# Staging of the weights before the first tile: double-buffered operand loads, two queues for the diagonal blocks, two weight matrices loaded later

## What is computed

```python
# layer 1: x = x + attn(layernorm(x))
mixed = silu(causal_depthwise_conv(x @ W_qkv.T, conv_w))      # K = 4 taps, 3072 channels
q, k, v = split(mixed);  z = x @ W_z.T
beta = sigmoid(x @ W_b.T);  g = -exp(A_log) * softplus(x @ W_a.T + dt_bias)
q = l2norm(q) / 8;  k = l2norm(k)
S = S * exp(g_t) + outer(k_t, v_t * beta_t);  o_t = q_t @ S    # per head, over time
out = (o * rsqrt(mean(o*o) + 1e-6) * silu(z)) @ W_out.T
# layer 2: x = x + ffn(layernorm(x))
def _unfold_tt(G1, G2):                                        # 512 x 512
    W = jnp.einsum('abcd,cefg->abefdg', G1, G2)
    return W.reshape(OUT_FEATURES, IN_FEATURES)
out_real = x_real @ W_real.T - x_imag @ W_imag.T + bias_real
out_imag = x_real @ W_imag.T + x_imag @ W_real.T + bias_imag
```

## Time and profile before

| what | us |
|---|---|
| runs (2): median, lowest, highest | 2968.16, 2960.76, 2975.57 |
| profiled execution: its own time | 2974.58 |
| its span on the slowest core (core 3) | 2973.0 |
| spans of the other cores | 2932.4 to 2961.1 |
| TensorE, matmuls busy | 1213.4 (41%) |
| VectorE (DVE) busy | 707.4 (24%) |
| ScalarE (ACT) busy | 342.2 (12%) |

### The profile page before, as it was taken

The page is one execution under the profiler, slowest core; times in us unless marked ns, Lnnn a source line. Parts: engine busy times, 40 slices in busy tenths (PEclk is TensorE's granted clock), DMA queues, the critical chain, the costliest instruction groups (busy, mean ns, idle before and its releaser), DMA issues.

```text
span 2973.0 us, 17447 instructions; the slowest of 8 cores (2932.4 to 2973.0 us)
## 1 busy us (share of the span) xinstructions
PE 1213.4 (41%) x5440; PEld 478.3 (16%) x5440; DVE 707.4 (24%) x1023; ACT 342.2 (12%) x570; POOL 131.1 (4%) x223
## 2 busy tenths in 40 slices
PE   0000072451634616614444733443852443762444
PEld 0000021211202213101122201111311111311111
DVE  0112312413214033022223022223112323202322
ACT  0000020020110201201110211111211111111111
POOL 1111100000000000000000000000000000000000
PEclk9999985655755657556566755665755666855656
DMA  9432202012030120121111101101011011012001
GB/s 162 64 85 92 88 18 22 18 39 8 22 29 18 39 1 18 47 5 18 18 18 39 23 25 4 35 19 39 11 36 6 18 34 34 13 41 5 18 18 25
DMA packets 138104, 94.79 MB, mean 32 GB/s; under 512 B 121003, under 2 KB 121776, under 8 KB 138016
## 3 DMA queue, kind: packets, MB, share of 16 engines
q0 software_dynamic: 44224, 39.15, 11.4%
q1 hardware_dynamic: 93792, 54.54, 6.7%
HBM read 99.76 MB, written 11.67 MB: 37 GB/s over the span
## 4 chain that ended last, share of the span: by engine, by line
PE 40%; DVE 19%; DMA 15%; ACT 10%; issue 8%; DVEq 3%; another core or an unknown queue 2%; POOL 2%; ACTq 0%; POOLq 0%; SPq 0%
PE ps L276 33%; DMA s_gamb<-scr 5%; PE psS L276 3%; DMA s_eaq<-scr 3%; ACT s_mixed L276 3%; PE psT L276 3%; DVE s_dsb L276 3%; DVE s_bn L276 3%; DVEq L275 2%; DVE s_Sall L276 2%; ACT L276 2%; DVE s_x2a L276 2%; ACT s_dsb L276 2%; DMA s_z<-p2i 2%
## 5 line engine op out<-in xcount | busy, mean ns | idle before, releaser
L276 PE MATMUL ps<-s_mixed,s_dwin 128*128 128x512 bf16 x640 | 296.6, 617 | 179.4 <-ACT s_mixed L276 141.8
L276 PE MATMUL ps<-s_lnxT,s_wqkvT 128*128 128x512 bf16 (+1 forms) x1344 | 300.9, 389 | 9.2 <-DVE s_lnxT L276 7.9
L276 PE MATMUL psT<-s_i128b,s_lnx 128*128 128x128 bf16 x256 | 32.4, 307 | 538.5 <-DVE s_lnx L276 538.5
L276 PEld LDWEIGHTS ps<-s_lnxT,s_wqkvT 128*128 128x128 bf16 x1344 | 133.2, 101 | 175.4 <-issue 37.4
L276 PE MATMUL psT<-s_i128b,s_mixed 128*128 128x128 bf16 x512 | 58.0, 283 | 205.4 <-DMA s_a<-s_dsb 83.7
L276 PE MATMUL psT<-s_i128b,s_gatedc 128*128 128x128 bf16 x256 | 32.4, 306 | 249.1 <-DVE s_Sbf L276 161.2
L276 PEld LDWEIGHTS ps<-s_mixed,s_dwin 128*128 128x128 bf16 x640 | 69.0, 126 | 403.7 <-issue 402.9
L276 ACT ACTIVATE s_mixed<-ps 128x512 bf16<-128x512 f32 x160 | 95.8, 598 | 328.4 <-PE ps L276 328.3
L276 DVE CAST s_mixed<-ps 128x512 bf16<-128x512 f32 (+1 forms) x88 | 57.9, 658 | 239.7 <-PE ps L276 239.7
L276 DVE COPY s_mixed<-s_halo 128x72 bf16<-128x72 bf16 x8 | 1.8, 228 | 465.9 <-ACT s_mixed L276 465.9
L276 PEld LDWEIGHTS psT<-s_i128b,s_lnx 128*128 128x128 bf16 x256 | 24.8, 138 | 545.4 <-issue 545.4
(11 more groups left out here) (115 smaller groups left out, 1185.2 us busy)
## 6 DMA issues: line engine op xcount, KB each, us to landing
s_dwin<-diagbf SPq DMA_DIRECT2D x160, 128.0 KB, 2.2
s_xa<-xpre SPq DMA_DIRECT2D x16, 512.0 KB, 3.8
s_xa<-xown SPq DMA_DIRECT2D x16, 512.0 KB, 4.7
s_xr<-xown SPq DMA_DIRECT2D x16, 512.0 KB, 4.6
s_wqkvT<-wqkvT POOLq DMA_DIRECT2D x1, 6144.0 KB, 45.1
s_z<-p1r POOLq DMA_DIRECT2D x16, 256.0 KB, 2.9
s_z<-p2r POOLq DMA_DIRECT2D x16, 256.0 KB, 3.0
s_z<-p1i POOLq DMA_DIRECT2D x16, 256.0 KB, 2.9
```

The source lines that it names most:

```text
L276: r = a(*args, **kw)
```

## The change

- Loads: `wzT` and `woutT` are taken out of the first block of loads. POOL issues them behind the weight product, on a semaphore of their own (`s_wz`), for which TensorE waits ahead of the first own tile.
- Diagonal blocks: the store of each group is issued by SP, which waits for the load (`s_dg`); POOL waits for the store (`s_dgm`) ahead of the next load. POOL no longer waits for VectorE there. SP's `xa` loads of tile 0 now stand behind the six stores. VectorE waits for the last store ahead of tile 0.
- Weight product: a second pair of operand buffers in `x2tc[1]`. The loads of step s+2 are issued when the product and sum of step s are done (`v_done[s]`), with one semaphore for each pair.

```diff
-    sG.inc(G_.dma_start(out=wzT[:]..., in_=d_wzT...), 16)
-    sG.inc(G_.dma_start(out=woutT[:]..., in_=d_woutT...), 16)
...
     for grp in range(6):
         p0 = grp * 16
-        sV.wait(G_)
-        sG.inc(G_.dma_start(
+        if grp > 0:
+            s_dgm.wait(G_)
+        s_dg.inc(G_.dma_start(
             out=dsb_t[:].rearrange("p (f c) -> p f c", f=16),
             in_=diag_flat[p0:p0 + 16].rearrange("f p c -> p f c")), 16)
-        G_.wait_ge(sG.h, sG.v)
-        sG.inc(G_.dma_start(
+        s_dg.wait(SY)
+        s_dgm.inc(SY.dma_start(
             out=diagbf_flat[p0:p0 + 16].rearrange("f p c -> p f c"),
             in_=dsb_t[:].rearrange("p (f c) -> p f c", f=16)), 16)
-        G_.wait_ge(sG.h, sG.v)
...
+    ffnbuf = [(z_chunk[:, 0:512], z_chunk[:, 512:1024]),
+              (x2tc[1][:, 0:512], x2tc[1][:, 512:1024])]
...
+    def ffn_issue(s):
+        dp1, dp2, kind, rc, cidx = steps[s]
+        b = s % 2
+        if s >= 2:
+            sV.wait(G_, v_done[s - 2])
+        s_fb[b].inc(G_.dma_start(out=ffnbuf[b][0],
+                            in_=dp1[cidx, rc * 128:(rc + 1) * 128, :]), 16)
+        s_fb[b].inc(G_.dma_start(out=ffnbuf[b][1],
+                            in_=dp2[cidx, rc * 128:(rc + 1) * 128, :]), 16)
+        g_done[s] = s_fb[b].v
+
+    ffn_issue(0)
+    ffn_issue(1)
+    for s, (dp1, dp2, kind, rc, cidx) in enumerate(steps):
+        b = s % 2
+        s_fb[b].wait(V_, g_done[s])
+        if cidx == 0:
+            sV.inc(V_.tensor_tensor(out=ffnACC, in0=ffnbuf[b][0],
+                                    in1=ffnbuf[b][1], op=ALU.mult))
+        else:
...
+        v_done[s] = sV.fence()
+        if s + 2 < len(steps):
+            ffn_issue(s + 2)
+        if cidx == 3:
...
+    s_wz.inc(G_.dma_start(out=wzT[:]..., in_=d_wzT...), 16)
+    s_wz.inc(G_.dma_start(out=woutT[:]..., in_=d_woutT...), 16)
+    wz_ready = s_wz.v
+    s_dgm.wait(V_)
...
     for tile in range(total_tiles):
...
+        if tile == n_pre:
+            s_wz.wait(T, wz_ready)
```

More of the change, by code:

```diff
@@ L232, in build_program @@
     cstp = sb("s_cst", [128, 4], F32)
+    markb = sb("s_mark", [1, 16])
     ps1 = es.enter_context(nc.psum_tensor("ps1", [128, 1024], F32))
@@ L251, in build_program @@
     s_spl = Sem(nc, es, "sspl")
+    s_dg = Sem(nc, es, "sdg")
+    s_dgm = Sem(nc, es, "sdgm")
+    s_fb = [Sem(nc, es, "sfb0"), Sem(nc, es, "sfb1")]
+    s_wz = Sem(nc, es, "swz")
     s_tap = Sem(nc, es, "stap")
@@ L301, in build_program @@
                         in_=d_wqkvT.rearrange("(dc p) c -> p dc c", p=128)), 16)
[L302 to L305, removed]
     sG.inc(G_.dma_start(out=wabT[:].rearrange("p (dc c) -> p dc c", dc=8),
@@ L350, in build_program @@
-    ffnP1 = z_chunk[:, 0:512]
-    ffnP2 = z_chunk[:, 512:1024]
+    ffnbuf = [(z_chunk[:, 0:512], z_chunk[:, 512:1024]),
+              (x2tc[1][:, 0:512], x2tc[1][:, 512:1024])]
     ffnACC = x2tc[0][:, 0:512]
     ffnTMP = x2tc[0][:, 512:1024]
[L354 to L370, removed]
+    steps = [(dp1, dp2, kind, rc, cidx)
+             for (dp1, dp2, kind) in ((d_p1r, d_p2r, "r"), (d_p1i, d_p2i, "i"))
+             for rc in range(4) for cidx in range(4)]
@@ new lines, in build_program @@
+    g_done = [0] * len(steps)
+    v_done = [0] * len(steps)
+    def ffn_issue(s):
[9 more added lines that the diff above has]
+    ffn_issue(0)
@@ new lines, in build_program @@
+    ffn_issue(1)
[6 more added lines that the diff above has]
+        else:
+            sV.inc(V_.tensor_tensor(out=ffnTMP, in0=ffnbuf[b][0],
+                                    in1=ffnbuf[b][1], op=ALU.mult))
+            sV.inc(V_.tensor_tensor(out=ffnACC, in0=ffnACC,
+                                    in1=ffnTMP, op=ALU.add))
+        v_done[s] = sV.fence()
+        if s + 2 < len(steps):
+            ffn_issue(s + 2)
+        if cidx == 3:
@@ L382, in build_program @@
     tap("wbig", wbig[:])
+    s_wz.inc(G_.dma_start(out=wzT[:].rearrange("p (dc c) -> p dc c", dc=8),
+                        in_=d_wzT.rearrange("(dc p) c -> p dc c", p=128)), 16)
+    s_wz.inc(G_.dma_start(out=woutT[:].rearrange("p (dc c) -> p dc c", dc=8),
+                        in_=d_woutT.rearrange("(dc p) c -> p dc c", p=128)), 16)
+    wz_ready = s_wz.v
+    s_dgm.wait(V_)
     total_tiles = (n_pre + n_own) if stage >= 2 else 0
@@ L869, in build_program @@
     G_.wait_ge(s_eaq.h, s_eaq.v)
+    SY.wait_ge(s_dg.h, s_dg.v)
+    SY.wait_ge(s_dgm.h, s_dgm.v)
+    SY.wait_ge(s_fb[0].h, s_fb[0].v)
+    SY.wait_ge(s_fb[1].h, s_fb[1].v)
+    SY.wait_ge(s_wz.h, s_wz.v)
     SY.wait_ge(s_dw[0].h, s_dw[0].v)
```

## The result

The changed kernel takes 2833.71 us (median of 11 runs, 2794.55 to 2872.96), the kernel before 2970.65 (10 runs). The ratio is 0.9465, with a 95% interval of 0.9418 to 0.9513; it leaves out the runs in which the cores of one die were slower than the others, and the two medians don't. The forecast was 2822 us in a range of 2798 to 2856, which is 0.951 of the 2968.2 that it started from. The profiled execution took 2815.64 us (forecast 2828.4), with a span of 2814.1 on its slowest core.

A forecast was written before the change was run, and what follows sets the result against it. The prediction held that staging before tile 0 (356.2 us), with TensorE idle, sets the end: entry 150.2 us earlier less 4 for token loads gives 146.2 less, 2828.4 profiled, 2822 us median, range 2798 to 2856.

The forecast's parts named there:

- Part 1: First loads: without `wzT`, `woutT` and the `xa` loads, the loads end at 49.9 us instead of 76.0.
- Part 2: VectorE's memsets (16.6 us): they lie beside the diagonal stage and end at about 66.5 us, cost 0.
- Part 3: Diagonal stage: first load landed at 55.3 us, stores of 4.5, six cycles of 11.9, sixth load landed at 114.8.
- the estimate from `dwin`'s transfer time: Diagonal store on SP's queue: `dwin`'s fixed part plus four times its transfer, 3.9 us.
- rival of slow stores: Diagonal stage: hardware queue slow with 2048 short pieces, stores of 8.8 us, 26 us more, 2848 us; chance 0.14.
- Part 4: Weight product: two overlapping chains, 2.84 us a step, 89.6 us in all, entry into tile 0 at 206.0 us.
- a group of four takes between 11.0 and 11.4: Weight product: four steps take 11.0 us with both chains free, 11.4 if the slower leads; 11.2 taken.
- no overlap: Weight product: the two buffers don't overlap, product stays at 177 us, gain 59, time 2909 us; chance 0.04.
- the exclusion beside multiplies: Weight product: POOL and VectorE exclude each other even for multiplies and sums, 11 us more, 2833 us; chance 0.08.
- Part 5: Tile 0's token loads beside the moved weight loads: third chunk 4 us late, with 0 and 11 as ends.
- Sum: Whole kernel: entry 150.2 us earlier less 4 for late token loads, 146.2 us less, median 2822 us.
- Everything behind the entry as long as before: From the entry into tile 0 to the end: no change in length apart from the third chunk's gap.

The follow-up runs named there:

- p3: Kernel before with only the loads of `wzT` and `woutT` moved behind the weight product: 2968.3 us (one execution), entry into tile 0 at 332.2 us.
- p2: Kernel before with only the diagonal stage changed (stores on SP's queue, no wait for VectorE): 2944.0 us (one execution), entry at 320.6 us.
- p1: Kernel before with only the two operand buffers of the weight product added: 2858.1 us (one execution), product 94.5 us.
- e4: Changed kernel with the `wzT` and `woutT` loads issued ahead of tile 1 instead of behind the product: product 96.2 us, mean entry 211.5 us.
- e1: Changed kernel with the conversions to bf16 after every fourth product step made by ScalarE instead of VectorE: product 95.5 us.
- e3: Changed kernel with the product's operand loads issued by SP on the hardware queue, still two pairs: product 82.3 us, entry at 225.4 us.
- b2: Changed kernel, product woven into the pre tiles' convolutions, small constants loaded first, `wqkvT`'s q columns behind the diagonal blocks: 2638.08 us, 0.8929 of before.
- e2: Changed kernel with four pairs of operand buffers for the product instead of two: 2775.1 us (one execution), product 65.9 us.

## Why the prediction was right

By its own steps, on the slowest core (forecast, then measured):

- **Part 1**, end of the loads at 49.9: 52.23, mean 51.5. The 24.3 us alone give 51.7, and p3, which moves only the weights, has 51.3 (mean). The token loads did leave, and `wqkvT` landed 2.9 us earlier. But the first diagonal load, now issued right behind the last constant, took most of that back: it runs beside the 3 KB for which VectorE waits, and holds them up. Over the cores they land 3.5 us behind the constant ahead of them, 3.0 in p2, where the diagonal load stands there too, and 1.2 in p3, where it doesn't. The step that failed is that a load's landing depends only on what is ahead of it in its queue.
- **Part 2**, memsets at no cost: yes, they end at 68.3, the first multiply is at 114.74.
- **Part 3**, first diagonal load landed at 55.3: 54.8, 6.4 us behind the last constant but one. Stores at 4.5: 3.8 to 4.1; the estimate from `dwin`'s transfer time (3.9) was the better one. Cycle 11.9: 11.3. First multiply at 116.4: 114.74. The rival of slow stores is refuted.
- **Part 4**, product 89.6: 98.3, the term that was mis-sized, by 8.7 us. p1, without late token loads and late weights beside it, has 94.5: 3.8 of the 8.7 come from neighbours. By the means over the cores, step 4 is multiplied 14.1 us after the first step, in p1 11.5, because the second pair of `s_z` took 6.2 us to land instead of 3.3: 2.6 us, beside the last store and the first two token loads on SP's queue, which no run tells apart. The last four steps take 13.0 us up to the entry, 12.0 in e4, where no weights follow: 1.0 us. The remaining 4.9 are in the step "a group of four takes between 11.0 and 11.4": it takes 11.8 in p1 (twelve cycles of the slower chain are 70.7 us apart on the slowest core, 5.89 each). The chain that has no step without a sum leads alone, which makes 11.4, and its loads land in 3.2 to 3.3 us over the cores, where those of the kernel before took 3.0. The rival "no overlap" is refuted, and so is the exclusion beside multiplies (e1).
- **Part 5**, third chunk 4 us late (its own figures, 11.5 - 7.9, give 3.6): 1.9, with a load of 9.5 us instead of 11.5. The rule of the Trainium skill (DMA: Bandwidth & Descriptors, "Queues, rings and completion order") that each engine alternates between the queues gave 0: the trace lies between, and e3 shows loads of SP's queue that took up to 25.7 us beside the same weights. What I had missed is that the weights also hold up the last operand pair, by 1.9 us on this core.
- **Sum**: entry 150.2 earlier, mean measured 146.5; less 1.9 for the chunk instead of 4. That this is so close is partly luck: by the means the first multiply came 60.9 us earlier (54.8 forecast) and the product shrank by 85.7 (95.4 forecast), errors of 6 and 10 us that cancel for the most part.
- **Everything behind the entry as long as before**: it is 9 to 13 us shorter, 10.5 of it in the wait for `s_gamb<-scr`, a term that the sum did not have and whose cause stays open. The ratio puts the time at 0.9465 x 2968.2 = 2809 us and the profiled execution at 2815.64, both 13 us below their forecasts; the median of all runs is 12 above.

## What to carry to other kernels

When TensorE idles at the start of a kernel, read the staging part like a path of its own: cut it at the waits, and what each cut is worth comes straight out of the rows, because nothing else hides it. Two buffers turn a chain of latency L into steps of L/2 at best (5.68 us for one step before, 5.65 to 5.9 for two after), and the chain with the longer steps sets the pace; before adding more, look at when the data are first needed, since work that moves behind the start is worth more than work that is made faster in it (0.947 against 0.893 here). A wait that is removed also lets go what stood behind it on its queue: in e3 two big loads that nobody needed yet went out early, and the product began 31 us later than in the changed kernel, of which 2 to 4 were expected without them.

## What the runs showed of the hardware

- A store of 512 KB in pieces of 256 bytes takes 3.8 to 4.1 us on SP's hardware queue, 4.8 on POOL's (after; before and p1).
- Big loads on POOL's queue hold up what SP's queue carries: beside 2 MB of q columns TensorE waited 10.4 us for one load of 128 KB (b2); beside two loads of 2 MB one of 256 KB took 25.7 us to land and a store of 512 KB 27.5, and SP's issuing instruction itself stood for 14.21 us (e3). It is not always so much: a token load of 512 KB beside the same 4 MB took 9.5 us (after) against 3.8 to 4.2 for the median one.
- A load of 3 KB landed 3.5 us behind the constant ahead of it (mean; 3.7 on the slowest core) when a bigger load of the same queue was under way behind it, and 1.2 us when there was none (after against p3). The last operand pair lost about 2 us to the weights behind it in the same way, on four cores of eight (after against e4).
- Four operand pairs in flight move 283 GB/s at 0.83 of the engines' time (e2); two pairs moved 184 at 0.58 (after).
- POOL's issue of a load takes 0.58 us beside a conversion of VectorE and 0.54 (mean) beside a multiply or beside nothing, and the load lands no later for it (3.20 against 3.23 us).
